# Shorter VectorE loop body, query factors turned in narrow transposes and moved as whole rows, and a new order of steps

## The chip, the cores and the metric

One core of one Trainium2 chip (trn2). The metric is device time in microseconds of one execution.

## The reference

x has 32 batches of 256 rows of 256 columns, the context 77 rows per batch. The first half is a cross attention of 8 heads of 128, without a softmax over keys: each head mixes a cosine similarity with a product of variance ratios, with weights that a small network takes from global means. The second half is a 16-head attention of head size 16 with a softmax, two normalisations and a gelu.

```python
dots = einsum('hqnd,hqmd->hqnm', f_q, f_k)
cosine_sim = dots / (qn[..., :, None] * kn[..., None, :])
q_ratio = 2.0 * minimum(q_var, 1.0) / (q_var + 1.0)
k_ratio = 2.0 * minimum(k_var, 1.0) / (k_var + 1.0)
var_component = einsum('hqn,hqm->hqnm', q_ratio, k_ratio)
mixed = cw * cosine_sim + vw * cosine_sim * decorr_scale + ww * var_component
out = einsum('hqnm,hqmd->hqnd', mixed, f_v)          # then @ w_out.T + b_out
x = x + tanh(g_xattn) * out
...
attn = softmax(scores)                                # 16 heads, over 256 rows
z = l2norm(l2norm(attn_out @ Wo) @ Wff)
x = x + tanh(g_ffn) * gelu(z)
```

## The kernel before, in words

A first phase (to about 235 us) prepares weights, context statistics and the mixing weights. The main phase (`main_phase`) works on 16 pairs of batches (512 rows each) in turns. Products of f32 values are made of three f16 matmuls (`products`, L861 to L863) on a high and a low half of each operand.

`ORDER` (L922) is a list of some 300 step names, written out by hand or by a program outside the kernel. Every engine walks through the same list and issues its own part of each step (`run`, with `a_part` and `b_part`). A turn has steps of three pairs: with `lead` 0 and 1 those of the first half and the projections, with `lead` 2 the softmax of the pair before. Turns 2 to 15 are one loop on the chip (`eng.Fori`, 14 turns, 13 branches back, line L1121); the turns at both ends are written out.

The steps that the text names:

- `q0`..`q7`: queries on TensorE; VectorE takes their statistics into `qst` (L1550, `bn_stats`).
- `qs1` (VectorE): moments of `qst` into `qft` (L871 to L882), variance ratios, times a weight, into `aux` (L1563). `qpow` (GpSimd, L1481): `rq`, inverse norms. `qs2` (VectorE, L1567): `rq` times a factor, into `aux`.
- `a0` (TensorE, L1286): one transpose of `aux`, 128x128. ScalarE copies 32 rows to `sqT` (L1394) and 32 to `wqT` (L1395), VectorE makes the low half of `wqT` (L1530).
- `aux` (SyncE, SP queue): stores `sqT` to DRAM as `sq_rows` (L1166), then loads `wqT` into one row group of `mT` in 8 small pieces (L1169).
- `sqe` (SP queue, L1178): 12 DMAs, each broadcasting a head's row of `sq_rows` over up to 77 partitions of `sqE`.
- `fk`, `G`, `V`: keys, keys times weights, values times weights; `.h` is the copy of the high half on ScalarE, `.l` the low half on VectorE.
- `d0`..`d5` (TensorE): dots. `d.o` (VectorE, L1580): `md` = dots times `sqE`. `m.h`, `m.l`: `mT`. `y0`, `y1`: the sum over keys; `y.o` adds x.
- `ln1`, `lpow`, `ln2` (`norm`, L1604), `zz`, `pq`, `pk`, `pv` (`v`, L1420): layer norm, transposes and projections of the second half. `ql`, `kl` are low halves on VectorE (L1537).
- `parts`, `back0`, `back1` (SP queue): q and k go to DRAM and come back stacked by heads as `qstack`, `kstack` (2 x 16 DMAs, L1205).
- `S` (TensorE, L1334), `M` (VectorE, L1624, row maxima `nm`), `X` (ScalarE, L1435, exponentials `prob` and their `sums`), 32 each a turn over three banks; `R` (VectorE: reciprocal `rs`, L1632, and `vsp`, L1638), `P` (TensorE, L1346), `E`, `L`, `O`, `F`: the rest of the attention. F4 (L1654) makes `zb`.

The results of all steps but S and P share three PSUM banks (`work`) in the turn of the list; a step waits until the bank's user three steps before has been drained (`wait_drained`, `wait_filled`).

Of the kernel before, what the change touches and what calls it, by code (L numbers as in the profile page):

```python
# [52 lines left out]
def build(nc, x, ctx_in, g_x, g_f, ln_g, ln_b, w_in, w_inT, w1T, b1, wln_g, wln_b, w2T, b2, w_outT, b_out,  # L53
# [812 lines left out]
def moments(nc, link, k0, st, ft, scale=1.0):  # L866
# [57 lines left out]
a0.h M5 S6 V2 X4 a0.l R0 aux M6 V1.h S7 P0 X5 V1.l M7 V2.h S8 X6 G3 M8 G4 V2.l X7 S9 V3 M9 G3.h ldx G4.h ldy G3.l X8
ldr R1 S10 V4 M10 V3.h G4.l X9 sqe V3.l S11 V5 V4.h M11 S12 X10 P1 V4.l M12 X11 S13 G5 M13 V5.h S14 G5.h fk0 V5.l E0
R2 X12 G5.l fk1 M14 X13 z fk0.h S15 P2 X14 M15 S16 S17 fk0.l d0 X15 M16 fk1.h M17 S18 X16 d1 fk1.l R3 X17 M18 S19 d2
L0 X18 M19 S20 P3 M20 X19 d0.o S21 S22 d1.o m0.h d3 M21 X20 m0.l d4 X21 R4 d2.o m1.h M22 S23 m2.h P4 E1 m1.l X22 m2.l
S24 d3.o d5 d4.o m3.h S25 zT0 M23 m4.h y0 m3.l zT0.h M24 X23 d5.o M25 m5.h X24 m4.l m5.l X25 S26 L1 S27 y1 M26 zT0.f
M27 X26 y0.o zT0.l X27 R5 R6 O0 y1.o ln1 S28 zT1 O0. S29 fk2 zT1.h P5 M28 lpow fk2.h zT1.f M29 P6 ln2 X28 S30 X29 S31
fk2.l zz0 M30 zz1 zz0.h zT1.l O1 zz1.h zz0.l X30 M31 q0 zz1.l X31 pk0 O1. R7 q0.o E2 P7 L2 pq0 E3 pk0.h L3 pk0.l pk1  # L930
pq0.h pq0.l pq1 pk1.h pk1.l O2 pq1.h pq1.l O3 O2. parts q1 O3. q2 F1 q1.o q3 q2.o back0 F2 q4 q5 q3.o F3 q4.o q6 q5.o
# [41 lines left out]
def main_phase(nc, ctx, w, x_rows, out_rows, rk_rows, kr_rows, sq_rows, fixed_rows, parts):  # L973
# [717 lines left out]
```

## Time and profile before

| | us |
|---|---|
| median of 3 runs | 1545.91 (1535.48 to 1546.38) |
| the profiled execution | 1539.16 |
| its span | 1537.4 |
| mean granted TensorE clock | 0.963 |
| busy: TensorE, VectorE, ScalarE, GpSimd | 1308.2, 1155.9, 1019.8, 199.5 |
| DMA | 125.05 MB in 182906 packets |

All times in rows are of the one profiled execution, from the start of its span. A row of the timeline gives the start, how long it took, the engine, line, operation and tile, and in brackets how long the engine was idle before it and what released it.

### The profile page before, as it was taken

The numbers are of one execution on the slowest core, as the hardware profiler recorded it, in microseconds if no ns is written. First come the engines' busy times: TensorE is split into PE (matmuls) and PEld (weight loads), VectorE is DVE, ScalarE is ACT, GpSimd is POOL, SyncE is SP. The second block draws the span as 40 slices with busy tenths as digits, with TensorE's granted clock in tenths as the row PEclk, the third lists the DMA queues.
The fourth block names the chain that finished last, engine by engine and source line by source line (L and its number), as shares of the span: only waits on it lengthen the run. The fifth ranks groups of instructions, "written<-read, shape, count | busy, mean of one in ns | idle before, by whom it ended". The sixth has DMA issues, their size and how long they took to land.

```text
span 1537.4 us, 35793 instructions
## 1 busy us (share of the span) xinstructions
PE 1308.2 (85%) x10706; PEld 868.5 (56%) x10706; DVE 1155.9 (75%) x3191; ACT 1019.8 (66%) x3381; POOL 199.5 (13%) x129
## 2 busy tenths in 40 slices
PE   5988756889898989898989898989898989898855
PEld 2655635465656565656565565656565656574622
DVE  5878465577877887878787787878787969696845
ACT  5564112276777777777777777768686868685767
POOL 2441031000101010101010101010101010101000
PEclk9999868999999999999999999999999999999978
DMA  8420002261616160716160807161616162626160
GB/s 255 139 91 17 3 10 63 53 107 40 134 38 134 33 138 28 138 33 137 34 131 13 148 24 144 28 138 34 126 46 115 56 111 61 111 61 111 49 110 15
DMA packets 182906, 125.05 MB, mean 81 GB/s; under 512 B 16430, under 2 KB 180431, under 8 KB 182800
## 3 DMA queue, kind: packets, MB, share of 16 engines
q1 hardware_dynamic: 182800, 124.00, 37.1%
q14 instruction: 84, 0.69, 0.2%
q8 instruction: 22, 0.36, 0.1%
HBM read 87.00 MB, written 25.77 MB: 73 GB/s over the span
## 4 chain that ended last, share of the span: by engine, by line
PE 32%; SPq 18%; DVE 12%; issue 12%; DMA 7%; ACT 3%; DVEq 0%; POOL 0%; POOLq 0%; ACTq 0%
PE work L861 9%; PE work L863 9%; PE work L862 9%; SPq L1178 7%; SPq L1169 5%; DMA sqE<-sq_rows 4%; SPq L1205 3%; DVE nm L1624 3%; PE attended L1346 2%; ACT prob L1435 2%; DMA qstack<-parts 2%; PE score L1334 2%; PE work L1241 1%; DVE l2s L1594 1%; DMA parts<-kl 1%
## 5 line engine op out<-in xcount | busy, mean ns | idle before, releaser
L1435 ACT ACTIVATE prob<-score,nm 128x256 f32<-128x256 f32 x1024 | 484.3, 514 | 30.9 <-DVE nm L1624 28.8
L1624 DVE TENSOR_REDUCE nm<-score 128x2 f32<-128x512 f32 x512 | 339.1, 682 | 36.8 <-PE score L1334 34.2
L1334 PE MATMUL score<-qstack,kstack 128*128 128x256 f16 x1024 | 193.8, 280 | 92.4 <-ACT prob L1435 45.9
L1435 ACT ACTIVATION_READ_ACCUMULATOR prob<-score,nm 128x1 f32 x1024 | 252.5, 247 | 0.0
L1334 PEld LDWEIGHTS score<-qstack,kstack 128*128 128x128 f16 x1024 | 80.0, 99 | 177.3 <-ACT prob L1435 111.1
L1550 DVE BATCH_NORM_STATS2 qst<-work 128x6 f32<-128x128 f32 x512 | 112.4, 284 | 68.7 <-PE work L863 68.7
L1346 PE MATMUL attended<-prob,vsp 128*32 128x256 f32 x2048 | 135.7, 388 | 1.4 <-DVE vsp L1638 1.4
L861 PE MATMUL work<-woutTh,fvph 128*128 128x256 f16 x384 | 105.8, 275 | 13.4 <-ACT v L1420 13.1
L1481 POOL TENSOR_TENSOR rq<-qft,mhalf 128x32 f32<-128x32 f32 x16 | 86.8, 5428 | 226.6 <-DVEq L1558 226.6
L861 PE MATMUL work<-xTh,Gh 128*128 128x256 f16 (+1 forms) x320 | 89.5, 280 | 28.3 <-DVE md L1580 28.3
L862 PE MATMUL work<-woutTl,fvph 128*128 128x256 f16 x384 | 105.5, 275 | 0.0
L863 PE MATMUL work<-woutTh,fvpl 128*128 128x256 f16 x384 | 105.5, 275 | 0.0
L1485 POOL TENSOR_TENSOR l2r<-l2v,mhalf 128x4 f32<-128x4 f32 x16 | 16.1, 1007 | 665.3 <-DVE l2v L1597 665.3
L861 PE MATMUL work<-wTh,xTh 128*128 128x512 f16 x256 | 98.1, 383 | 3.9 <-DVE xTl L1544 1.9
L862 PE MATMUL work<-wTl,xTh 128*128 128x512 f16 x256 | 98.0, 383 | 0.0
L863 PE MATMUL work<-wTh,xTl 128*128 128x512 f16 x256 | 98.0, 383 | 0.0
L1388 ACT ACTIVATE Vph<-work,rkc 128x256 f16<-128x256 f32 (+1 forms) x160 | 73.9, 525 | 30.5 <-PE work L863 30.5
L862 PE MATMUL work<-xTl,Gh 128*128 128x256 f16 (+1 forms) x320 | 89.4, 280 | 0.0
L863 PE MATMUL work<-xTh,Gl 128*128 128x256 f16 (+1 forms) x320 | 89.3, 279 | 0.0
L861 PE MATMUL work<-Vph,mTh 128*128 128x256 f16 (+1 forms) x320 | 87.3, 273 | 1.6 <-issue 0.2
L863 PE MATMUL work<-Vph,mTl 128*128 128x256 f16 (+1 forms) x320 | 87.1, 272 | 0.0
L862 PE MATMUL work<-Vpl,mTh 128*128 128x256 f16 (+1 forms) x320 | 87.0, 272 | 0.0
(327 smaller groups left out, 3288.9 us busy)
## 6 DMA issues: line engine op xcount, KB each, us to landing
kstack<-parts SPq DMA_DIRECT2D x256, 64.0 KB, 4.0
qstack<-parts SPq DMA_DIRECT2D x256, 64.0 KB, 4.2
sqE<-sq_rows SPq DMA_DIRECT2D x64, 154.0 KB
s_xin<-in_x SPq DMA_DIRECT2D x8, 1024.0 KB, 6.0
xin<-in_x SPq DMA_DIRECT2D x16, 512.0 KB, 3.4
x2S<-in_x SPq DMA_DIRECT2D x16, 512.0 KB, 4.7
x<-x2S SPq DMA_DIRECT2D x16, 512.0 KB, 4.1
out<-zb SPq DMA_DIRECT2D x16, 512.0 KB, 5.2
```

The costliest lines, as they stand in the source:

```text
L861: nc.tensor.matmul(out, a["h"][at], b["h"][bt], start=first, stop=False)
L862: nc.tensor.matmul(out, a["h"][at], b["l"][bt], start=False, stop=False)
L863: return nc.tensor.matmul(out, a["l"][at], b["h"][bt], start=False, stop=last)
L1169: sp.dma_start(mT[half][KR_ROW:KR_ROW + H, t // 2, HT - 1, t % 2 * P:(t % 2 + 1) * P], wqT[half][(PT + t) * H:(PT + t + 1) * H, :]).then_i ...
L1178: sp.dma_start(sqE[lo:hi, t, :].rearrange("p (t n) -> p t n", n=P), sq_rows[:, h, :].partition_broadcast(hi - lo)).then_inc(sq_in, 16)
L1334: last = nc.tensor.matmul(sc[n % SC][:, jj * NQ:(jj + 1) * NQ], kstack[:, e, j, b2 * NQ + k * P:b2 * NQ + (k + 1) * P], qstack[:, j, b2 * ...
L1346: last = nc.tensor.matmul(pvb[t][32 * j:32 * j + 32, 0:NQ], vsp[:, e, k, j, :], prob[:, n % PG, k, j, :], start=(e == 0 and k == 0), stop= ...
L1388: last = nc.scalar.activation(dst, src, ACT.Copy, scale=scale)
L1435: nc.scalar.activation(prob[:, g % PG, k, u % 4, :], sc[n % SC][:, jj * NQ:(jj + 1) * NQ], ACT.Exp, bias=nm[:, u:u + 1], accum_out=sums[:, ...
L1481: nc.gpsimd.tensor_tensor(rq[:], qft[:, 0, :, :], w["mhalf"][:].rearrange("p (t h) -> p t h", h=H), ALU.pow).then_inc(rq_ready, 1)
L1550: last = nc.vector.bn_stats(qst[:, t, 4 * half + h, :], bank(e)[:, h * DH:(h + 1) * DH])
L1624: nc.vector.tensor_reduce(nm[:, 2 * n:2 * n + 2], sc[n % SC][:, :].rearrange("p (u q) -> p u q", q=NQ), AX.X, ALU.max, negate=True).then_i ...
```

## The change

- Waits that VectorE's, GpSimd's and other engines' own order already covers are left out: of several names in `wait_drained` the last only, `sq_in` and `y_in` once a pair, `init` once. One copy in `moments` and its link go, and `rs` is written over `sums`. VectorE's loop body goes from 318 to 307 instructions, and the instructions written ahead of it become 6 fewer (counted in the two built programs).
- `aux` has two planes instead of four, and a plane is turned by 4 transposes of [128x8] into [8 x 512]: `a1` for the ratios (`wqT`), `a0` for the factors (`sqT`). `sqT` and `wqT` have 8 partitions of 512 values instead of 32 of 128.
- `sq_rows` is [8, 512]: a broadcast reads one piece of 2 KB for each partition instead of four of 512 bytes. The 8 small loads of `wqT` become 2, in a step `wq` of their own.
- A new `ORDER`, with 47 users of the three banks instead of 46.

```diff
-    sq_rows = nc.dram_tensor("sq_rows", (PT, H, P), F32, kind="Internal").ap()
+    sq_rows = nc.dram_tensor("sq_rows", (H, PR), F32, kind="Internal").ap()
...
-    link(k0 + 4, nc.vector.tensor_copy(ft[:, 5, :, :], ft[:, 1, :, :]))
...
-    aux, sqT, wqT = sb("aux", [P, 4, PT, H]), sb("sqT", [PT * H, P]), pair("wqT", [2 * PT * H, P])
+    aux, sqT, wqT = sb("aux", [P, 2, PT, H]), sb("sqT", [H, PR]), pair("wqT", [H, PR])
...
                     sp_wait_drained(a, "a0")
-                    sp_wait_filled(a - 1, "y0", "y1")
-                    sp.dma_start(sq_rows.rearrange("t h n -> (t h) n"), sqT[:]).then_inc(sq_stored, 16)
+                    sp_wait(sq_in, a * SQ_LOADS * 16)
+                    sp.dma_start(sq_rows, sqT[:]).then_inc(sq_stored, 16)
+                elif step == "wq":
+
+                    sp_wait_drained(a, "a1")
+                    sp_wait_filled(a - 1, "y1")
                     for half in "hl":
-                        for t in range(PT):
-                            sp.dma_start(mT[half][KR_ROW:KR_ROW + H, t // 2, HT - 1, t % 2 * P:(t % 2 + 1) * P],
-                                         wqT[half][(PT + t) * H:(PT + t + 1) * H, :]).then_inc(wq_in, 16)
+                        sp.dma_start(mT[half][KR_ROW:KR_ROW + H, :, HT - 1, :],
+                                     wqT[half][:].rearrange("h (b n) -> h b n", b=2)).then_inc(wq_in, 16)
...
-                            sp.dma_start(sqE[lo:hi, t, :].rearrange("p (t n) -> p t n", n=P),
-                                         sq_rows[:, h, :].partition_broadcast(hi - lo)).then_inc(sq_in, 16)
+                            sp.dma_start(sqE[lo:hi, t, :], sq_rows[h, :].partition_broadcast(hi - lo)).then_inc(sq_in, 16)
...
-                    pe.wait_ge(wqr_ready, a + 1)
-                    pe.wait_ge(sq_ready, a + 1)
-                    last = nc.tensor.transpose(bk[:, 0:P], aux[:].rearrange("p s t h -> p (s t h)"), ident[:])
+                    pe.wait_ge((sq_ready, wqr_ready)[c], a + 1)
+                    for t in range(PT):
+                        last = nc.tensor.transpose(bk[0:H, t * P:(t + 1) * P], aux[:, c, t, :], ident[:])
...
-                    wait_drained(dve, a, *(f"q{n}" for n in range(2 * PT)))
-
-                    wait_filled(dve, a - 1, "a0")
-                    dve.wait_ge(init, 5)
+                    wait_drained(dve, a, f"q{2 * PT - 1}")
+
+                    wait_filled(dve, a - 1, "a1")
...
-                    dve.wait_ge(sq_in, a * SQ_LOADS * 16 + SQ_LOADS * 16)
+                    if c == 0:
+                        dve.wait_ge(sq_in, a * SQ_LOADS * 16 + SQ_LOADS * 16)
```

The head of the list and its tail, before and after:

```diff
-rk qs1 V0 qpow S0 G0 V0.h M0 S1 S2 G0.h G1 M1 X0 V0.l X1 G0.l S3 G2 M2 G1.h S4 M3 V1 G2.h X2 G1.l G2.l X3 qs2 S5 M4 a0
+rk V0 qs1 G0 V0.h S0 qpow V1 G0.h M0 V0.l X0 G0.l S1 V1.h a1 M1 S2 S3 a1.h M2 G1 X1 V1.l G1.h M3 V2 ldr X2 a1.l S4
...
-q7 q6.o pv0 q7.o F4 pv1 pv0.v res pv1.v out back1
+q4 q3.o q5 q4.o q6 q5.o F4 q7 q6.o res pv1 back1 q7.o pv1.v out
```

On the SP queue, at the start of the loop body (behind the loads of `back1` of the turn before), the store of `sqT` and what stands between it and the broadcast. Before:

```order
L1166 DMA sq_rows<-sqT 32x128
L1169 DMA mTh<-wqTh 8x128 x4
L1169 DMA mTl<-wqTl 8x128 x4
L1156 ISA
L1156 DMA xin<-in_x 128x4x256
L1139 REGISTER_ALU
L1161 ISA
L1161 DMA x2S<-in_x 128x4x256
L1184 ISA
L1184 DMA Vph<-kr_rows 8x2x256
L1184 ISA
L1184 DMA Vpl<-kr_rows 8x2x256
```

After:

```order
L1185 ISA
L1185 DMA Vph<-kr_rows 8x2x256
L1185 ISA
L1185 DMA Vpl<-kr_rows 8x2x256
L1138 ISA x2
L1165 DMA sq_rows<-sqT 8x512
L1138 REGISTER_ALU
L1138 ISA
L1180 DMA sqE<-sq_rows 77x512
```

The loads of x and of `wqT` now stand behind the 12 broadcasts, the `kr_rows` loads ahead of the store.

On VectorE, the end of what stands ahead of the first `md` of a turn (ISA and REGISTER_ALU set registers for waits). Before:

```order
L1621 TENSOR_TENSOR oTl<-attended,oTh 128x256
L1623 REGISTER_ALU
L1624 TENSOR_REDUCE nm<-score 128x2
L1623 REGISTER_ALU
L1624 TENSOR_REDUCE nm<-score 128x2
L1049 REGISTER_ALU
L1574 ISA
L1579 ISA
L1580 TENSOR_TENSOR md<-work,sqE 128x512
```

After:

```order
L1641 TENSOR_TENSOR vsp<-v,sums 128x8x16
L1626 REGISTER_ALU
L1627 TENSOR_REDUCE nm<-score 128x2
L1048 ISA
L1576 ISA
L1581 ISA
L1582 TENSOR_TENSOR md<-work,sqE 128x512
```

In the whole turn 21 row maxima (`nm`) stand ahead of the first `md` before, 15 after.

On ScalarE, the end of the exponentials (`prob`) of a turn. Before:

```order
L1435 ACTIVATE prob,sums<-score,nm 128x256 x2
L1452 ACTIVATE junk,nrm<-work 128x256 x2
L1454 ACTIVATE zb<-work 128x256
L1049 REGISTER_ALU
L1441 ACTIVATE oTh<-attended 128x256
L1438 REGISTER_ALU
L1441 ACTIVATE oTh<-attended 128x256
L1049 REGISTER_ALU
L1405 REGISTER_ALU
L1407 ACTIVATE kh<-work 128x512
```

After:

```order
L1437 ACTIVATE prob,sums<-score,nm 128x256 x2
L1407 REGISTER_ALU
L1409 ACTIVATE kh<-work 128x512
L1048 REGISTER_ALU
L1409 ACTIVATE kh<-work 128x512
L1048 REGISTER_ALU
L1443 ACTIVATE oTh<-attended 128x256
```

The group of O1 (`junk`, `zb`) went ahead of the last exponentials, and both `kh` stand right behind them, since TensorE computes pk0, pk1 and pq0 ahead of P7.

## Rows read from the trace of the kernel before

**Rows 1.** Table by stretches: 13 turns of the loop, then one turn's two parts.
```profile
384.40:1402.70 1018.30, 922.11 (x8023) 614.58 (x8021) 814.12 (x2186) 752.23 (x2561) 108.39 (x65) 0.99 0.40 84
...
core 0: us, PE busy (x) PEld busy (x) DVE busy (x) ACT busy (x) POOL busy (x), PEclk, DMA share, GB/s
1020.90:1071.60 50.70, 46.22 (x461) 33.74 (x462) 46.40 (x106) 44.85 (x166) 4.50 (x2) 1.00 0.34 63
1071.60:1099.20 27.60, 24.39 (x157) 13.24 (x155) 16.23 (x63) 13.05 (x33) 3.86 (x4) 1.00 0.49 121
```
**Rows 2.** Waits, of the turn 1013.4 to 1091.6; the last row of the whole span.
```profile
PE score L1334 <- ACT prob L1435: 2.9, 4, 1.8
PE work L861 <- DVE md L1580: 1.5, 1, 1.5
PE work L861 <- ACT v L1420: 0.9, 1, 0.9
PE work L1241 <- DVE norm L1604: 0.5, 1, 0.5
...
DVE qft L871 <- issue: 50.4, 13, 4.2
```
**Rows 3.** Timeline of the hand-over between two turns.
```profile
1045.52 1.07 PE L1346 MATMUL attended<-prob,vsp 128*32 128x256 f32 x16
...
1071.04 0.47 ACT L1435 ACTIVATE prob<-score,nm 128x256 f32<-128x256 f32 x1
1071.95 0.29 DVE L1638 TENSOR_TENSOR vsp<-v,rs 128x128 f32<-128x128 f32 x1
1074.20 0.59 ACT L1407 ACTIVATE kh<-work 128x512 f16<-128x512 f32 x1
1078.51 0.69 DVE L1537 SCALAR_TENSOR_TENSOR ql<-work,qh 128x512 f16<-128x512 f32 x1 [0.60 <-ACT qh L1407]
1096.95 0.39 PE L1334 MATMUL score<-qstack,kstack 128*128 128x256 f16 x2 [2.14 <-DMA qstack<-parts]
1099.17 0.47 ACT L1435 ACTIVATE prob<-score,nm 128x256 f32<-128x256 f32 x1 [0.62 <-DVE nm L1624]
```
**Rows 4.** The chain to `md`: tile, DMA, queue and timeline, 1020 to 1050.
```profile
L1394 ACT ACTIVATE sqT<-work x1: 267/267/267, 1025.6 to 1025.6; 32x128 f32<-32x128 f32 x1
DMA to landing us min/median/max: 3.9/3.9/3.9
...
DMA packets 3097, 1.75 MB, mean 146 GB/s; under 512 B 137, under 2 KB 3097, under 8 KB 3097
q1 hardware_dynamic: 3097, 1.75, 52.6%
...
1035.98 7.74 SPq L1178 DMA_DIRECT2D sqE<-sq_rows  x12
1043.38 4.73 DMA sqE<-sq_rows
1048.23 1.29 DVE L1580 TENSOR_TENSOR md<-work,sqE 128x512 f32<-128x512 f32 x2 [1.62 <-DMA sqE<-sq_rows]
```
**Rows 5.** Timeline of VectorE behind the branch.
```profile
1017.28 0.21 DVE L871 TENSOR_TENSOR qft<-qst 128x32 f32<-128x32 f32 x1 [3.92 <-issue]
1019.99 0.19 DVE L1563 TENSOR_TENSOR aux<-qft,wwv 128x32 f32<-128x32 f32 x1
```
**Rows 6.** Timeline of ScalarE behind the same branch.
```profile
1014.53 1.28 ACT L1388 ACT_TABLE_LOAD   x1
```
**Rows 7.** Timeline of VectorE where the loop is left.
```profile
1404.46 0.21 DVE L871 TENSOR_TENSOR qft<-qst 128x32 f32<-128x32 f32 x1
```
**Rows 8.** DMA queues: packets, MB, share; the span, the turn, 1089.2 to 1089.7.
```profile
q14 instruction: 84, 0.69, 0.2%
...
q14 instruction: 5, 0.04, 0.3%
...
q14 instruction: 1, 0.01, 14.3%
```
**Rows 9.** The chain of waits in the hand-over, two of its steps.
```profile
1079.36 0.22 PE work L862
...
1089.07 0.22 PE work L862
```

More of the change, by code:

```diff
@@ L913 @@
 SC_CREDIT = SCORES
-A_STEPS, B_STEPS = 12, GROUPS + 5
+A_STEPS, B_STEPS = 11, GROUPS + 5
 ORDER = """
-rk qs1 V0 qpow S0 G0 V0.h M0 S1 S2 G0.h G1 M1 X0 V0.l X1 G0.l S3 G2 M2 G1.h S4 M3 V1 G2.h X2 G1.l G2.l X3 qs2 S5 M4 a0
[L924 to L931, printed above, removed]
-q7 q6.o pv0 q7.o F4 pv1 pv0.v res pv1.v out back1
+rk V0 qs1 G0 V0.h S0 qpow V1 G0.h M0 V0.l X0 G0.l S1 V1.h a1 M1 S2 S3 a1.h M2 G1 X1 V1.l G1.h M3 V2 ldr X2 a1.l S4
+V2.h qs2 S5 G1.l X3 a0 V2.l G2 M4 G3 a0.v M5 G2.h S6 aux X4 V3 R0 M6 G3.h G2.l X5 S7 P0 M7 V3.h G3.l G4 X6 sqe V3.l S8
+G5 G4.h M8 S9 X7 V4 G4.l M9 X8 R1 S10 X9 S11 M10 P1 G5.h X10 G5.l S12 V5 M11 ldy V4.h M12 S13 wq d0 X11 V4.l ldx V5.h
+M13 S14 X12 d1 V5.l R2 X13 M14 S15 P2 d0.o X14 M15 S16 m0.h d1.o fk0 M16 m0.l S17 fk0.h d2 E0 fk0.l d3 X15 M17 m1.h
+d2.o S18 X16 d4 m1.l M18 X17 R3 S19 d5 m2.h M19 X18 S20 m2.l P3 d3.o X19 d4.o fk1 m3.h M20 m3.l X20 S21 S22 z y0 m4.h
+fk1.h d5.o L0 m5.h M21 E1 R4 X21 M22 zT0 S23 m4.l X22 P4 fk1.l zT0.h m5.l S24 y0.o S25 y1 zT0.f M23 L1 X23 M24 M25 X24
+R5 X25 zT0.l zT1 y1.o O0 zT1.h ln1 S26 O0. S27 P5 zT1.f M26 lpow O1 M27 X26 ln2 X27 S28 S29 M28 O1. zz0 zz1 zT1.l
+zz0.h S30 R6 fk2 zz1.h zz0.l X28 P6 zz1.l fk2.h M29 S31 pk0 M30 X29 M31 X30 fk2.l pk1 X31 pq0 pk0.h R7 pk1.h pk0.l P7
+E2 pq0.h pk1.l L2 pq1 pq0.l E3 L3 O2 pq1.h pq1.l O3 O2. parts q0 O3. q1 F1 q0.o pv0 q1.o back0 F2 q2 pv0.v q3 q2.o F3
+q4 q3.o q5 q4.o q6 q5.o F4 q7 q6.o res pv1 back1 q7.o pv1.v out
 """.split()
@@ L1186, in a_part @@
                 elif step == "parts":
-                    sp_wait_drained(a, "pq0", "pq1", "pk0", "pk1")
+                    sp_wait_drained(a, "pq1", "pk1")
                     for landed in stack_in:
@@ L1469, in _ @@
             nc.gpsimd.memset(kstack[:], 0.0).then_inc(init, 1)
-            nc.gpsimd.memset(aux[:], 0.0).then_inc(init, 1)
             def a_part(e, a):
@@ L1525, in a_part @@
                     drain(last, e)
-                elif e == "a0" and part == "l":
+                elif e == "a1" and part == "l":
                     done = HALVES[lead(e)]
                     dve.wait_ge(hi_ready[lead(e)], a * len(done) + done.index(e) + 1)
-                    rows = slice(PT * H, 2 * PT * H)
-                    drain(nc.vector.scalar_tensor_tensor(wqT["l"][rows, :], bank(e)[rows, 0:P], MS, wqT["h"][rows, :],
+                    drain(nc.vector.scalar_tensor_tensor(wqT["l"][:], bank(e)[0:H, :], MS, wqT["h"][:],
                                                          ALU.mult, ALU.subtract), e)
@@ L1628, in b_part @@
                     units = slice(8 * n, 8 * n + 8)
-                    if n == 0:
+                    if n == 0 and isinstance(b, int) and b == 0:
                         dve.wait_ge(init, 3)
                     dve.wait_ge(exp_done, b * 2 * SCORES + 8 * n + 8 + EXP_CREDIT)
-                    link(n + 1, nc.vector.reciprocal(rs[:, units], sums[:, units]))
+                    link(n + 1, nc.vector.reciprocal(sums[:, units], sums[:, units]))
                     if n == 0:
-                        wait_drained(dve, b, "pv0", "pv1")
+                        wait_drained(dve, b, "pv1")
                     dve.wait_ge(pv_done, b * GROUPS + n - 1 + PV_CREDIT)
```

65 lines of the change are left out of this document (34 added, 31 removed).

## The prediction

> **What bounds the kernel now.** The page's shares (TensorE 85% busy, VectorE 75%, ScalarE 66%) are averages over unlike stages, so the table by stretches comes first [rows 1]. The 13 turns between the first and the last branch of the main loop take 1018.3 us, 78.3 us a turn; divided by 13, TensorE is busy 70.9 us of it, VectorE 62.6, ScalarE 57.9. TensorE's clock is granted at 0.99 of full speed, 2.4 GHz, there. No engine is full, yet the turn splits into two unlike parts: from the first to the last exponential of a turn (50.7 us) ScalarE works 44.85 us and TensorE 46.2; from the last exponential to the first of the next turn (27.6 us) ScalarE works 13. The turn is thus a loop of two stretches: a dense one, in which TensorE and ScalarE are both nearly full, and a hand-over.
>
> The table of waits of one turn [rows 2] names what opens the gaps on TensorE: 2.9 us for exponentials, 1.5 for `md`, 0.9 for ScalarE's `v`, 0.5 for `norm`, and in the timeline 2.1 for the stacked queries (qstack) [rows 3]. VectorE waits 1.6 us for `sqE` [rows 4] and, in the timeline, 3.9 us for nothing ("issue") from 1013.37 on, before it begins the statistics `qft` at 1017.28 [rows 5]. That is the loop's branch. ScalarE takes the same branch without a gap: its table load, the first work of a new turn, has no idle time before it [rows 6]. When VectorE leaves the loop instead of branching back, the same `qft` begins with no idle time either [rows 7]. So the 3.9 us belong to the taken branch on VectorE alone; 13 of them sum to 50.4 us [rows 2].
>
> **Does the shorter program remove that stall?** In a turn 5 instruction packets arrive, of about 8.2 KB (0.69 MB in 84) [rows 8]. A narrow window places one just before VectorE's branch at 1089.2 to 1089.7 [rows 8]. Counted along VectorE's instructions in the trace, it lies at the 314th of the 318 of the loop, and another at the 186th, 128 apart. My reading: the body just reaches into a fourth block of 128 instructions, whose entry pushes the first block out. The new body has 307 instructions, and 6 went ahead of it, so the boundary should fall at the 320th, behind the end. All 5 packets a turn would go: the 84 should fall to about 20.
>
> The Trainium skill (Runtime: NRT & Kernel Launch, section on instruction fetch) has a store of 512 instructions, refilled in blocks of 256, and a branch out of the two-block window fetches. The trace agrees with the kind of stall but not with the block, since its packets are 8.2 KB. By blocks of 256, 307 instructions could still straddle three, and nothing would change; that is the first rival, whose time is worked out there from rows.
>
> **The edits and their price, for one turn.**
> (1) Stall and copy. `qft` to `aux` took 2.9 us [rows 5]; one copy of about 0.2 goes. All of it then runs while TensorE computes V0 and G0. Now the first exponential stands 2.25 us behind the first score (1096.95 to 1099.17), because the row maximum waits behind `qft` [rows 3, 5]; score 0.4, maximum 0.68 and hops give 1.35. Gain 0.9 us. The rest of the stall was covered: the first score waits for qstack until 1096.95 anyway, which is why 3.9 us removed are not 3.9 us gained.
> (2) Tail order. From the end of the last exponential (1071.51) to the end of `ql` (1079.20) it is 7.7 us, as TensorE then still has P7, three projections and their evacuations before it [rows 3]. In the new order pk0, pk1 and pq0 run before P7, and ScalarE's copies follow the exponentials at once. What is left behind the last exponential: `vsp` ready after 0.7, P7 1.0, pq1 (6 matmuls of 0.216; 45 such stand between the two rows of the chain [rows 9]) 1.3, copy 0.6, residual 0.7, hops 0.2 [rows 3]: 4.5 us. Gain 3.2. From `ql` to the first score 17.75 us pass [rows 3]: 4 stores, their landing, 16 loads at 0.45, the last landing. Nothing in it changes. From the end of pq1 TensorE has O2, O3, q0 to q7 (60 matmuls at 0.216), pv0, pv1 and V0 (39 of half the columns, 0.108) and G0 (0.6) to do, 17.8 us; `ql` ends 1.4 us behind pq1, so qstack comes at 19.2 and TensorE waits 1.4 us, where it waited 2.1 and 0.9 for `v` [rows 2, 3].
> (3) Added in the dense stretch: one square-and-copy group (O1) moves into it, 1.2 us of ScalarE (two squares, two reads, a copy, each 0.2 to 0.4); the two copies of 0.27 us on 32x128 become two of [8x512], not seen before, bounded by 0.27 and by the 0.6 of a 128x512 copy [rows 3, 4]; I take 0.6, as free length is what it has in common: +0.6. Together +1.8. Four narrow transposes instead of one, twice, cost TensorE some 0.3 to 0.9 us; it has that much idle behind the exponentials at this place.
> (4) The chain to `md`. Now: store of sqT, eight small loads, two of x, two of kr, then 12 issues for `sqE` from 1035.98, last landing 1048.11, `md` 1048.23, 34.9 us behind the end of `zb` [rows 4]. New, from the end of pv1 on TensorE: the SP queue is through its 16 loads, `out` and two kr loads at about 12; sqT is copied at about 11.8, behind four pairs of exponentials and six evacuations; its store lands 3.9 later [rows 4], at 16. Then 12 `sqE` issues. They took 12.1 us to the last landing, in packets of 512 B; new rows are 2 KB. From below: no issue held up (half of the 7.74 us of now, 4) and the last landing of 4.7 as now, 8.7 [rows 4]. From above: no gain, 12.1; that no packet of 2 KB was seen leaves this end open, and rival B takes it up. I take 10, nearer to above since the bytes are the same. So `sqE` stands at 26, between 25 and 28.5. But the order asks for it sooner: 15 maxima come before the first `md`, not 21, and I put that at 25 (first score 3.6, first exponential 1.35 later, 14 pairs at the 0.95 that two steps of `prob` take, 6.7 of evacuations). The wait is 1 to 1.5, where it was 1.6 to 2.0 [rows 4]: gain 0.5. The eight small loads and the x loads leave this chain; that pays for the earlier place.
> The Trainium skill (DMA: Bandwidth & Descriptors, section on why a DMA increments by 16) says that a DMA runs on the largest number up to 16 that divides its outer dimension. With 77, 51, 76 rows the load is uneven, and by that rule one DMA engine moves 84 of the rows. The trace shows only the average: 3097 packets and 52.6% of 16 engines over 12 us, 0.033 us each [rows 4]. By the rule 84 rows of four such packets take 11 us, between my value and the upper end; what a packet of 2 KB takes, no run here shows yet.
> (5) Waits dropped on other engines, `rs` written over `sums`, one memset less: nothing; they are waits already met, hidden under busy engines. If one was not redundant in time, another wait of the same chain stands in its place.
> (6) `norm` to zz0: 5.0 us of TensorE work cover it where 5.5 did, so its gap of 0.5 [rows 2] grows to 1.0: loss 0.3 (half falls into ScalarE's work).
>
> (7) The wait of 0.9 for `v` at V0 goes with the 47th bank user; it lies beside the wait for qstack: 0 by itself. But ScalarE has 5.85 us idle in the dense stretch [rows 1], 2 of them at `md`; banks that come free earlier and a first exponential that no longer lags can return between 0 and 2 of the rest, and I count 0.5.
>
> Sum for a turn: -0.9 - 3.2 + 1.8 - 0.5 + 0.3 - 0.5 = -3.0. The profiled execution took 1539.16 us with a span of 1537.4; 14 turns give 42, the turns at the edges another 2: 1495. The runs shown (1535 to 1546, median 1545.9) lie 4 to 7 us around and above that execution, so a median of 1497 is my figure. One per cent, 15 us, is about what a measurement here can tell from no change.
>
> **Rivals.**
> A. The stall stays, because a boundary still falls inside the new body. `qft` then ends 6.6 us behind pv1 and not 2.8, the first maximum 2.5 us late: -3.0 + 2.5 = -0.5 a turn, 1532. For it: the positions are inferred. Against: 13 instructions of room. Chance 0.09. The block rule quoted above leads here.
> B. Slower: the chain to `md`. If the broadcast of 2 KB rows out of one DRAM row took longer than the 12.1 us of now, every us beyond 10 is a us of turn, since VectorE stands at `md` with the maxima behind it and ScalarE starves. The gain of 3.0 is eaten at 13 us, slower by 1% at 14.1; at 16 it costs +3.0, 1581. For it: `md` is asked for six maxima earlier, and the store leaves from 8 partitions, not 32. Against: same bytes, a fourth of the packets. 0.05.
> C. Order gives back: `sqE` at 28.5 (+3 of wait), or the last exponentials, now after pk0 and pk1, hold P7: -0.5 to -1.3 a turn, about 1524. 0.16.
> D. More: ScalarE's other idle time in the dense stretch shrinks by its full 2 instead of 0.5, and half of the cost in (3) is covered as well: -5, 1467. 0.16.
> My forecast, -2 to -4 a turn (1482 to 1510): 0.54.
>
> Range: 1466 to 1532, from D to A. Faster by over 1% (below 1523): forecast, D and half of C, 0.78; within 1%, A and the other half of C: 0.17; slower, B: 0.05.
>
> **What would show it.** VectorE idle "issue" before `qft` gone; instruction packets near 20, none in a turn; the first exponential 1.4 us behind the first score; `ql` 4.5 us behind the last exponential; `sqE` landed about 10 us behind its first issue, `md` waiting about 1 us. Turns of 75.3 us. I am wrong if `qft` still waits, if `md` waits over 3 us, or if the dense stretch grows by more than 2 us.

## The result and the profile after

The changed kernel takes 1453.36 us (median of 4 runs, 1447.33 to 1455.04), the kernel before 1541.24 us beside it (4 runs, 1535.48 to 1546.38): ratio 0.9424, 95% interval 0.9372 to 0.9475. The forecast was 1497 us in a range of 1466 to 1532: the sign was right, the size was not, and the time lies below the range. The profiled execution took 1452.54 us, with a span of 1450.8.

The page of the changed kernel, busy times and DMA queues:

```profile
PE 1305.6 (90%) x10818; PEld 878.3 (61%) x10818; DVE 1138.5 (78%) x3171; ACT 1023.9 (71%) x3381; POOL 199.1 (14%) x128
...
q1 hardware_dynamic: 151392, 124.00, 30.8%
q8 instruction: 22, 0.36, 0.1%
q14 instruction: 19, 0.16, 0.0%
```

TensorE and ScalarE do the same work as before; what went is idle time. Queue q14 has 19 packets where it had 84 [rows 8].

The table by stretches: the 13 turns of the loop, then the dense stretch and the hand-over of one turn (us, busy time of each engine, granted clock, DMA share, GB/s):

```profile
375.06:1324.69 949.63, 917.20 (x8114) 622.78 (x8113) 806.37 (x2172) 756.16 (x2561) 108.41 (x65) 1.00 0.34 90
963.66:1013.80 50.14, 47.80 (x481) 35.36 (x479) 46.20 (x106) 46.38 (x171) 4.39 (x2) 1.00 0.27 71
1013.80:1036.30 22.50, 22.50 (x148) 12.62 (x146) 15.82 (x62) 11.77 (x28) 3.92 (x4) 1.00 0.44 134
```

Against [rows 1]: a turn takes 949.63 / 13 = 73.05 us instead of 78.33. In the hand-over TensorE is now busy all of 22.50 us, where it had 3.2 us of gaps in 27.60. In the dense stretch ScalarE is busy 1.5 us longer than before (46.38 against 44.85) in a stretch that is 0.6 shorter: its idle time fell from 5.85 to 3.76 us. This turn is a good one: over the 13 turns ScalarE's busy time there rose from 44.8 to 46.4 us and its idle time fell from 5.9 to 4.1.

Waits of one turn (959.5 to 1032.2), then of the whole span the wait of `md`:

```profile
PE work L861 <- DVE Vpl L1525: 0.8, 1, 0.8
PE score L1335 <- ACT prob L1437: 0.6, 2, 0.5
PE work L1242 <- DVE norm L1607: 0.5, 1, 0.5
PE work L861 <- DVE md L1582: 0.4, 1, 0.4
```

```profile
DVE md L1582 <- DMA sqE<-sq_rows: 16.7, 13, 2.4
```

Against [rows 2]: 2.9 for exponentials became 0.6, 1.5 for `md` 0.4, and the waits for `v` and `qstack` are gone. A wait of 0.8 for `Vpl`, the low half of V on VectorE, is new. `norm` did not grow to the 1.0 that step 6 of the prediction feared. The row `qft <- issue` has gone from the waits.

The timeline of VectorE at the branch, and of the hand-over:

```profile
958.35 1.68 DVE L1550 BATCH_NORM_STATS2 qst<-work 128x6 f32<-128x128 f32 x8
960.15 0.21 DVE L871 TENSOR_TENSOR qft<-qst 128x32 f32<-128x32 f32 x1
...
1013.28 0.49 ACT L1437 ACTIVATE prob<-score,nm 128x256 f32<-128x256 f32 x1
1013.73 1.11 ACT L1409 ACTIVATE kh<-work 128x512 f16<-128x512 f32 x2
1014.83 1.07 PE L1347 MATMUL attended<-prob,vsp 128*32 128x256 f32 x16
1017.97 0.69 DVE L1537 SCALAR_TENSOR_TENSOR ql<-work,qh 128x512 f16<-128x512 f32 x1 [1.00 <-ACT qh L1409]
```

`qft` follows `qst` at once, where it stood 3.92 us idle [rows 5]. `kh` follows the last exponential at once, and `ql` ends 4.9 us behind it, not 7.7 [rows 3].

These steps, as means over the 13 turns (from the starts and lengths of the instructions named, in the timeline of each turn), beside the forecast by the prediction's own terms:

| us | before | forecast | after |
|---|---|---|---|
| end of last exponential to end of `ql` | 7.70 | 4.5 | 4.89 |
| end of `ql` to first score | 17.64 | 17.75 | 16.43 |
| first score to first exponential | 2.33 | 1.35 | 1.23 |
| first to last exponential | 50.66 | 51.8 | 50.51 |
| turn | 78.33 | 75.3 | 73.05 |

The first and third line came nearly as forecast. The second and fourth hold the missing 2.3 us a turn. The rest of the miss lies outside the 13 turns: of the 86.6 us that the two profiled executions differ by, 13 turns hold 68.7, one more turn of the loop 5.3, and the edges 12.7, where the prediction had 2.

### The profile page after: what moved, and what is told of

Its sections match the earlier page's. It is cut to its first block, busy times and chain, and to the rows that moved or that the text cites. A ratio compares the mean times of both kernels' runs of the same rounds, so it can differ in the third digit from the quotient of the medians.

```text
span 1450.8 us, 35577 instructions
## 1 busy us (share of the span) xinstructions
PE 1305.6 (90%) x10818; PEld 878.3 (61%) x10818; DVE 1138.5 (78%) x3171; ACT 1023.9 (71%) x3381; POOL 199.1 (14%) x128
## 4 chain that ended last, share of the span: by engine, by line
PE 38%; DVE 18%; issue 14%; ACT 6%; DMA 5%; SPq 3%; DVEq 1%; POOL 1%; ACTq 0%; POOLq 0%
PE work L861 10%; PE work L863 10%; PE work L862 10%; DVE nm L1627 5%; DMA sqE<-sq_rows 4%; PE attended L1347 4%; ACT prob L1437 3%; DVE mTl L1537 3%; PE score L1335 2%; SPq L1180 2%; DVE md L1582 2%; PE work L1242 1%; DVE l2s L1597 1%; DVE norm L1607 1%; DVE norm L1518 1%
## 5 line engine op out<-in xcount | busy, mean ns | idle before, releaser
L1437 ACT ACTIVATE prob<-score,nm 128x256 f32<-128x256 f32 x1024 | 473.2, 480 | 44.6 <-DVE nm L1627 40.4
L1437 ACT ACTIVATION_READ_ACCUMULATOR prob<-score,nm 128x1 f32 x1024 | 216.7, 212 | 0.0
L1335 PE MATMUL score<-qstack,kstack 128*128 128x256 f16 x1024 | 186.0, 277 | 28.4 <-ACT prob L1437 19.2
L1347 PE MATMUL attended<-prob,vsp 128*32 128x256 f32 x2048 | 139.4, 390 | 4.0 <-DVE vsp L1641 3.2
L1335 PEld LDWEIGHTS score<-qstack,kstack 128*128 128x128 f16 x1024 | 86.6, 98 | 87.7 <-ACT prob L1437 55.5
L861 PE MATMUL work<-woutTh,fvph 128*128 128x256 f16 x384 | 105.0, 273 | 13.7 <-DVE Vpl L1525 12.7
L1422 ACT ACTIVATE v<-work 128x512 f32<-128x512 f32 x32 | 19.1, 597 | 130.4 <-PE work L863 130.4
L1347 PEld LDWEIGHTS attended<-prob,vsp 128*32 128x32 f32 x2048 | 53.9, 110 | 56.9 <-DVE vsp L1641 17.4
## 6 DMA issues: line engine op xcount, KB each, us to landing
s_xin<-in_x SPq DMA_DIRECT2D x8, 1024.0 KB, 6.0
```

The costliest lines, as they stand in the source:

```text
L861: nc.tensor.matmul(out, a["h"][at], b["h"][bt], start=first, stop=False)
L1335: last = nc.tensor.matmul(sc[n % SC][:, jj * NQ:(jj + 1) * NQ], kstack[:, e, j, b2 * NQ + k * P:b2 * NQ + (k + 1) * P], qstack[:, j, b2 * ...
L1347: last = nc.tensor.matmul(pvb[t][32 * j:32 * j + 32, 0:NQ], vsp[:, e, k, j, :], prob[:, n % PG, k, j, :], start=(e == 0 and k == 0), stop= ...
L1437: nc.scalar.activation(prob[:, g % PG, k, u % 4, :], sc[n % SC][:, jj * NQ:(jj + 1) * NQ], ACT.Exp, bias=nm[:, u:u + 1], accum_out=sums[:, ...
```

## Experiments

Medians of the kernel before beside these runs were 1538.9 to 1540.9 us; ratios are to it, with their 95% intervals.

### The stall of VectorE: where the code lies, or how long it is

**Only the waits of VectorE's program left out** (order, layout and the rest as before; body of 311 instructions).

```diff
-                    dve.wait_ge(sq_in, a * SQ_LOADS * 16 + SQ_LOADS * 16)
+                    if c == 0:
+                        dve.wait_ge(sq_in, a * SQ_LOADS * 16 + SQ_LOADS * 16)
```

and the same for `q0` to `q7`, `y_in` and `init`. Expected:

> The kernel before, with only the waits left out of VectorE's program that its own order covers (loop body 311 instructions instead of 318, 2 fewer ahead of it); order, layout of aux and all else as before. Theory of the prediction (step 1 less its copy): the 3.9 us of issue idle before qft go, 84 instruction packets fall to about 20, and of the 3.9 us about 0.9 a turn come back as time, since the first score waits for qstack anyway: 13 us less, ratio about 0.99. Rival: the stall holds the whole hand-over (VectorE late at qft, at the maxima and at the banks behind them), 2.5 to 3.9 us a turn: 35 to 50 us less, ratio 0.977 to 0.967.

Measured: 1523.01 us, ratio 0.9898 (0.9866 to 0.9929); q14 19 packets, no issue idle before `qft`. It gains 16 us, 1.2 a turn: the prediction's 0.9 was near, the rival's 2.5 to 3.9 was not. Of the 1.2, 0.8 lie between the first score and the first exponential, where the prediction had them, and 0.6 ahead of the first score (17.05 us behind `ql` instead of 17.64); the dense stretch takes 0.2 back.

**60 instructions ahead of the loop of the kernel before, the loop itself untouched.**

```diff
+            for _ in range(120):
+                dve.wait_ge(init, 1)
             run(dve, a_part, b_part)
```

(Two such waits share one instruction; the built program has 60 more.)

> The kernel before with nothing changed inside the loop: 60 instructions that only wait for something long done are put ahead of VectorE's loop. Theory of the block: the stall hangs on where the 318 instructions lie against boundaries 128 apart; 60 more ahead move the boundaries from the 58th, 186th and 314th to the 126th and 254th, the body no longer reaches a fourth block: issue idle before qft gone, instruction packets about 20, time as in e1_prune within 5 us. Rival of the length: a body of 318 is too long wherever it lies: 3.9 us of idle before qft and 84 packets stay, time as before, up to 4 us more for the 60 instructions.

Measured: 1520.98 us, ratio 0.9899 (0.9864 to 0.9935), the same gain as with the shorter body. Of its page:

```profile
q14 instruction: 20, 0.16, 0.0%
```

With 318 instructions in the body and 60 more ahead, the stall is gone. It hangs on where the body lies, not on how long it is.

**16 and 8 instructions ahead of the loop of the changed kernel**, by the same edit with 32 and with 16 waits:

> The changed kernel with nothing changed inside the loop: 16 instructions that only wait for something long done go ahead of VectorE's loop. Theory of the block: 64 + 16 + 307 = 387 instructions pass the boundary at 384, the stall comes back: idle of 3 to 4 us before qft in each turn, 4 to 5 instruction packets a turn (about 84 in all), and the time grows by what a stall costs in the new order, 2.5 us a turn as the prediction priced it (35 us, ratio to the changed kernel 1.024). Rival of the length: 307 fits wherever it lies: no stall, at most 1 us more.

> As the run with 16 ahead, but 8 instructions: 64 + 8 + 307 = 379, under the boundary at 384. Theory of the block: no stall, about 20 packets, the time of the changed kernel within 2 us. Rival (any added instruction, or another place in the store, disturbs it): an idle before qft and tens of us more here too.

Measured with 16: 1480.76 us, ratio 0.9644 (0.9599 to 0.9689). With 8: 1447.32 us, ratio 0.9408 (0.9379 to 0.9437), no more than the changed kernel's time. The queue on the page and the group of `qft`, with 16 ahead:

```profile
q14 instruction: 84, 0.69, 0.2%
```

```profile
L871 DVE TENSOR_TENSOR qft<-qst 128x32 f32<-128x32 f32 x16 | 3.5, 217 | 31.8 <-PE work L863 23.2 <-issue 8.4
```

and the same group in the changed kernel:

```profile
L871 DVE TENSOR_TENSOR qft<-qst 128x32 f32<-128x32 f32 x16 | 3.5, 218 | 1.8
```

All 84 packets are back with 16, none with 8 (19). So a boundary lies where it was counted. The prediction put it at the 320th instruction, which is 384 behind a boundary that lies 64 instructions ahead of the body: 64 + 16 + 307 passes 384, 64 + 8 + 307 does not. The row with 31.8 us also shows how a releaser is misread: it names TensorE for 23.2 of them, though the same edit with 8 instructions ahead leaves next to no idle there; TensorE's last release only fell into the time in which VectorE stood. The stall costs more in the new order, (1480.76 - 1453.36) / 14 = 2.0 us a turn, because nothing covers it any more: the first score no longer waits for qstack, and the first exponential stands 3.43 us behind it instead of 1.23.

### Order, and the pieces of sq_rows

**The tail of the order turned back** (pk0, pk1 and pq0 behind the last exponentials and P7):

```diff
-P6 zz1.l fk2.h M29 S31 pk0 M30 X29 M31 X30 fk2.l pk1 X31 pq0 pk0.h R7 pk1.h pk0.l P7 E2 pq0.h pk1.l L2 pq1 pq0.l E3 L3 O2
+P6 zz1.l fk2.h M29 S31 M30 X29 M31 X30 fk2.l X31 pk0 R7 E2 P7 L2 pq0 E3 pk0.h L3 pk0.l pk1 pq0.h pq0.l pq1 pk1.h pk1.l O2
```

> The changed kernel with one edit in its order: pk0, pk1 and pq0 go back behind the last exponentials and P7, as before. Prediction's step 2: the end of the last exponential to the end of ql grows from 4.9 to about 7.7, all of it on the path: 2.8 us a turn, 39 us more in all. Rival: qstack no longer ends the hand-over in the changed kernel, it lands about 1.5 us before TensorE asks for it; then 2.8 later costs 1.3 a turn, 18 us, and the first score waits for qstack again.

Measured: 1492.53 us, ratio 0.9697 (0.9662 to 0.9732); 39 us more than the changed kernel. `ql` ends 7.83 us behind the last exponential, and from there the first score comes 16.42 behind as before the edit. That is what step 2 of the prediction says of the tail, nearly to the number. The rival falls: 16.4 us is TensorE's own work between pq1 and the first score (17.8 less the 1.4 by which `ql` follows pq1, as the prediction counted), and it all starts later when pq1 does.

**sq_rows in pieces of 512 bytes**:

```diff
-    sq_rows = nc.dram_tensor("sq_rows", (H, PR), F32, kind="Internal").ap()
+    sq_rows = nc.dram_tensor("sq_rows", (PT, H, P), F32, kind="Internal").ap()
...
-                            sp.dma_start(sqE[lo:hi, t, :], sq_rows[h, :].partition_broadcast(hi - lo)).then_inc(sq_in, 16)
+                            sp.dma_start(sqE[lo:hi, t, :].rearrange("p (t n) -> p t n", n=P),
+                                         sq_rows[:, h, :].partition_broadcast(hi - lo)).then_inc(sq_in, 16)
```

> The changed kernel with sq_rows in pieces of 512 bytes, as before, under the same store and the same 12 broadcasts at the same place. Prediction's term: first issue to last landing about 11 us with 2 KB rows, 12.1 with 512 bytes: md waits 1 us longer, 1 us a turn, 14 us more in all. Rival 1 (the packets count, not the bytes: issues of 0.64 instead of 0.35 us and four times the packets): 3 us a turn or more, over 40 us. Rival 2: nothing, within 3 us, as the bytes are the same and the wait at md is hidden.

Measured: 1469.6 us, ratio 0.9555 (0.9525 to 0.9585), 16 us more, 1.2 a turn. The wait of `md`, to set beside 16.7:

```profile
DVE md L1583 <- DMA sqE<-sq_rows: 34.2, 14, 3.9
```

From the first issue to `md` it is 12.6 us with 512 bytes and 11.3 with 2 KB (means of 13 turns): the term that the prediction put at 10 and expected to be 12.1 with 512 bytes.

**Everything but the order** (the order of before, with a0 split into a1 and a0, and `wq` behind `aux`):

```diff
-rk qs1 V0 qpow S0 ... X3 qs2 S5 M4 a0 a0.h M5 S6 ... a0.l R0 aux M6
+rk qs1 V0 qpow S0 ... X3 qs2 S5 M4 a1 a0 a1.h a0.v M5 S6 ... a1.l R0 aux wq M6
```

> The changed kernel (shorter VectorE program, aux in two planes, narrow transposes, 2 KB rows) with the order of before: only a0 becomes a1 and a0 side by side, and the step wq stands right behind aux. The prediction's steps: stall and copy -1.2 a turn by the run e1_prune, sqE earlier by 1 to 2 us where md waits 1.6 to 2.0 (-1.5), two longer copies +0.6: about -2.1 a turn, 1510 us, and the order gives the rest, 3 to 4 us a turn. Rival of the layout: it gives more than half of the 5.3, below 1495 us. The 16 loads of qstack and kstack landed 4.1 us (median) behind their issue before and 2.9 in the changed kernel, for no reason seen so far: if the layout (tiles at other addresses) does it, the median is 2.9 here; if the order does it, 4 to 5.

Measured: 1498.74 us, ratio 0.9734 (0.9697 to 0.9771), 24 us less than with the shorter program alone, and between the expected 1510 and the rival's 1495. No step of the prediction holds such a gain for the layout. The group of the stack loads gave the hint, here before, then this run:

```profile
DMA to landing us min/median/max: 2.7/4.2/6.9
```

```profile
DMA to landing us min/median/max: 2.2/3.0/3.9
```

### The addresses of the stacks

The 16 loads of a half stack write rows of 512 bytes into qstack and kstack. In the kernel before these tiles begin at 173696 and 181888 bytes of a partition, 128 past a multiple of 256; in the changed kernel, since `aux`, `sqT` and `wqT` have other sizes, at 176384 and 184576, which are multiples of 256. DMA queues during the loads of the first half, 1085.5 to 1094.0 before and 1024.0 to 1031.2 after:

```profile
q1 hardware_dynamic: 2137, 0.97, 73.8%
```

```profile
q1 hardware_dynamic: 2120, 0.97, 46.9%
```

The same 0.97 MB in the same number of packets: 8.5 us x 16 engines x 0.738 / 2137 = 0.047 us a packet before, 7.2 x 16 x 0.469 / 2120 = 0.025 after.

**Tiles moved, in the kernel before and in the changed one.** Four runs, of which nothing but addresses changes:

```diff
+    sb("shift", [P, 544])                       # 2176 bytes, ahead of x2S
+    sb("shift", [P, 32])                        # or 128 bytes, ahead of qstack
+    sb("shift", [P, 512])                       # or 2048 bytes, ahead of qstack
```

and in the changed kernel `rq` (128 bytes) moved from ahead of x2S to behind kstack.

> The kernel before with an unused tile of 2176 bytes a partition ahead of x2S, so that x2S, qh to kl, v, qstack, kstack, prob and what follows lie 2176 bytes higher; nothing else. If the addresses are what made the last 8 loads of a stack slow (packets of 512 bytes took 60 to 90 ns there, 27 in the changed kernel) and the exponentials slower (514 against 480 ns), this changes the landing median of 4.1 us or the mean of prob. If the order or what runs beside does it: landing, prob and time as before within noise.

> The kernel before with 128 unused bytes a partition right ahead of qstack: qstack and kstack start at a multiple of 256 bytes (173824, 182016) instead of 128 past one, and x2, prob and what follows move by 128 too; qh to kl stay where they were. Theory of alignment to 256 bytes: it is enough; the packets of 512 bytes of the last 8 loads fall from 60 to 90 ns to about 27, landing median 2.8 to 2.9 us, ql to the first score 15.5 instead of 17.6, time -15 to -20 us as with the 2176 bytes. Rival (a large shift does it, or the source tiles qh to kl do): packets, landing and time as before.

> The kernel before with 2048 unused bytes ahead of qstack: qstack and kstack move far but stay 128 past a multiple of 256. Theory of alignment: nothing changes, packets of 60 to 90 ns, landing median 4.1 or more, time as before within 5 us. Rival (the place in memory, whatever its alignment): packets of 27 ns and 15 to 20 us less.

> The changed kernel with rq (128 bytes) moved behind kstack: x2S, qh to kl, v, qstack and kstack start 128 bytes lower, so 128 past a multiple of 256 as in the kernel before; nothing else changes. Theory: the slow packets return, qstack lands some 17.1 to 17.7 us behind ql instead of before 16.4, the first score waits for it, and of the 1.4 us a turn that the prediction had there 0.7 to 1.4 come back: 11 to 22 us more, about 1465 to 1475 us. Rival: the new order hides it, within 5 us of the changed kernel.

| kernel | stacks past a multiple of 256 | us | ratio to before |
|---|---|---|---|
| before, 2176 bytes ahead of x2S | 0 | 1519.74 | 0.988 (0.985 to 0.9909) |
| before, 128 bytes ahead of qstack | 0 | 1525.52 | 0.9929 (0.9893 to 0.9965) |
| before, 2048 bytes ahead of qstack | 128 | 1539.05 | 0.9998 (0.998 to 1.0017) |
| changed, rq behind kstack | 128 | 1500.74 | 0.9765 (0.9736 to 0.9794) |

Landing of the stack loads, first 128 bytes, then 2048 bytes:

```profile
DMA to landing us min/median/max: 2.2/2.8/3.8
```

```profile
DMA to landing us min/median/max: 2.6/4.2/6.1
```

A shift of 128 bytes does it, one of 2048 does not: of these places it is the ones at a multiple of 256 bytes that are fast. Whether the tiles qh to kl, moved too by the 2176 bytes, add to it stays open; the two intervals overlap.

The last run is the telling one: the whole change with unaligned stacks takes 1500.74 us, 47 more than the changed kernel. The forecast was 1497, but 1465 to 1475 was expected of this run, so the size of the loss was a surprise. Its loss does not lie at the first score (16.68 us behind `ql` instead of 16.43), where the prediction had looked. First the DMA queues during the loads of the second half (990 to 996: share of the engines in 40 slices, then the queue), then the timeline of the SP queue behind them and of `md`:

```profile
DMA  9999999999999999999999999999999999999999
...
q1 hardware_dynamic: 1583, 0.72, 127.1%
```

```profile
997.24 0.28 SPq L1165 DMA_DIRECT2D sq_rows<-sqT  x1
1001.56 4.31 SPq L1180 DMA_DIRECT2D sqE<-sq_rows  x12
...
1012.97 0.69 DVE L1582 TENSOR_TENSOR md<-work,sqE 128x512 f32<-128x512 f32 x1 [3.68 <-DMA sqE<-sq_rows]
```

The same chain in the changed kernel:

```profile
970.07 0.28 SPq L1165 DMA_DIRECT2D sq_rows<-sqT  x1
971.75 4.23 SPq L1180 DMA_DIRECT2D sqE<-sq_rows  x12
...
982.83 0.69 DVE L1582 TENSOR_TENSOR md<-work,sqE 128x512 f32<-128x512 f32 x1 [0.72 <-DMA sqE<-sq_rows]
```

All DMA engines are full (packets overlap in the record, hence 127%) with the slow loads of the second half. The store of sqT is queued behind them and lands 4.3 us later (997.24 to 1001.56) instead of 1.7, `sqE` starts later by as much, and `md` waits 56.4 us in the span instead of 16.7:

```profile
DVE md L1582 <- DMA sqE<-sq_rows: 56.4, 14, 5.2
```

Over the 13 turns `md` comes 3.2 us later behind the first store of q and k, and a turn takes 3.4 us more (76.42).

**The order of before with unaligned stacks**, to see whether the two gains add:

```diff
-    rq = sb("rq", [P, PT, H])
...
+    rq = sb("rq", [P, PT, H])
     x2 = sb("x2", [P, PT, DIM])
```

> All edits but the order, with rq moved behind kstack so that the stacks keep their place 128 past a multiple of 256: stall, copy, aux layout and 2 KB rows without order and without alignment. If alignment is what e5_old_order gained beyond the stall (1499 against 1523): the time is 1515 to 1522 us here, and the order alone, at equal alignment, is worth 15 to 21 us (to 1501) instead of 47. Rival: alignment pays only in the new order, and this stays near 1500.

Measured: 1529.2 us, ratio 0.9931 (0.991 to 0.9952). With the three others:

| us | stacks 128 past | stacks aligned |
|---|---|---|
| order of before | 1529.2 | 1498.7 |
| new order | 1500.7 | 1453.4 |

The two do not add: alignment gives 30 us in the old order and 47 in the new one, the order 28 or 45. The layout by itself, unaligned and in the old order, gains nothing over the shorter program alone (1529.2 against 1523.0, with intervals that just overlap): the wait at `md` falls from 25.9 to 3.4 us in the span, but the dense stretch grows from 50.87 to 52.48 us a turn. Half of that is work: ScalarE is busy 45.5 us there instead of 44.7, as the two longer copies of step 3 would have it (`sqT` takes 0.57 us instead of 0.27). Beside it stands a wait that is new. In both runs that have all edits but the order, TensorE stands once a turn for 3.1 us at a V step of the dense stretch, some 8 us behind the first exponential:

```profile
PE work L861 <- DVE Vpl L1525: 50.9, 18, 3.1
```

With the shorter program alone this wait is 3.8 us in the span, in the changed kernel 12.7. The old order has the two transpose steps side by side, and so one more user of the three banks, without room made for it; that this is why TensorE waits is argued, not tested. If so, part of the 28 us of the order is room that it makes for the layout. The rival (alignment pays only in the new order) falls; the expected 1515 to 1522 was too low as well.

**Reciprocals over sums in the kernel before**, for the exponentials, which take 480 ns instead of 514 in the changed kernel:

```diff
-                    link(n + 1, nc.vector.reciprocal(rs[:, units], sums[:, units]))
+                    link(n + 1, nc.vector.reciprocal(sums[:, units], sums[:, units]))
```

> The kernel before with the reciprocals written over sums instead of into rs; nothing else. The exponentials took 514 ns and the reading of their sum 247 in the kernel before, 490 and 223 with all edits but the order, 480 and 212 in the changed kernel, and moving tiles did not change them. If rs matters (ScalarE adds into sums while VectorE reads it): below 500 and 235 here, and up to 1 us a turn less. Otherwise 512 to 516 and 245 to 248 and the time of before; the cause is then another edit and stays open.

Measured: 1537.61 us, ratio 0.9985 (0.9964 to 1.0006), exponentials 514 ns. It is not this, nor the alignment (514 with 128 bytes ahead), nor the 512-byte pieces (478). The cause stays open.

**A version that beats both.** In the changed kernel `sqE`, `md` and x2S still begin 64, 64 and 32 bytes past a multiple of 256. Small tiles given out in another order align them at no cost in space:

```diff
+    rk_all, l2m, st4 = sb("rk_all", [P, HT, NB]), sb("l2m", [P, PT, 2]), sb("st4", [P, PT, 2])
     sqE, md = sb("sqE", [P, HT, PR]), sb("md", [P, 2, PR])
...
+    l2s, l2t = sb("l2s", [P, PT, 6]), sb("l2t", [P, PT, 2])
+    l2v, l2r = sb("l2v", [P, PT]), sb("l2r", [P, PT])
+    x2S = sb("x2S", [P, PT, DIM])
```

> The changed kernel with tiles given in another order so that sqE, md and x2S too start at a multiple of 256 bytes (before this at 64, 64 and 32 past one); qstack and kstack stay where they are. If alignment matters for each DMA that writes there: 2 KB packets of sqE fall from 105 to 120 ns, md waits 0.5 to 1 us a turn less than its 1.2, the time falls by 5 to 14 us. Rival: only short packets, or loads that stand close together, suffer: packets and time as in the changed kernel within 3 us.

Measured: 1440.13 us, ratio 0.937 (0.9345 to 0.9396), 13 us less than the changed kernel, with a turn of 72.42 us.

```profile
DVE md L1583 <- DMA sqE<-sq_rows: 8.2, 10, 2.8
```

The time and the wait (0.6 us a turn less) are as expected, the packets only in part. While `sqE` alone is on the queues its packets of 2 KB take 106 ns with either address. Where the load of x2S runs beside it, packets of 1 KB fall from 68 to 61 ns and those of 2 KB from 119 to 110 (packets that overlap one of the other size, means of 13 turns), and `md` comes 0.5 us earlier behind the first issue. Three tiles moved at once; which of them pays, no run parts.

## Why the prediction was wrong in size

**Step 1, stall and copy (-0.9 a turn).** Right in kind and nearly in size: 16 us alone, 1.2 a turn. The limit of three blocks of 128, inferred from two packets, held in six placements: counted from the boundary ahead of it, the body ends at 388 and 387 in the two kernels that stall (before, and changed with 16 ahead), and at 379, 320, 371 and 379 in the four that do not. The Trainium skill (Runtime: NRT & Kernel Launch, section on instruction fetch) has blocks of 256 in a store of 512. The placements alone do not rule these out: if the body of before began not 70 but 198 behind a boundary, it would end at 516 there, at 515 with 16 ahead, and at 507 or less in the others. What the trace does not fit is the block. Every packet has 8192 bytes; in the loop they come one at a time, the 186th and the 314th instruction of the body get one each, and 5 come in a turn, an odd number. The block of 128 is shown by that, the limit of three such blocks is argued. The lag of the first exponential in the turn read was 2.22 us and not the 2.25 of the sum, which changes nothing. That the stall would be worth 2.0 in the new order was priced at 2.5 in rival A, nearly right too.

**Step 2, tail of the order (-3.2).** Right: -2.81, and 39 us back when it is undone. But the sentence behind it failed: "From `ql` to the first score 17.75 us pass ... Nothing in it changes", and so "TensorE waits 1.4 us". It is 16.43 us, and TensorE does not wait. Its own work was counted rightly (17.8, less the 1.4 by which `ql` follows pq1) and now sets the time. What was wrong is the arrival of `qstack`, taken from the trace of before as if it were fixed. There the first score, which waited for it, stood 17.64 us behind `ql`; it stands 17.05 behind with VectorE's shorter program alone and 16.54 with all edits but the order and the alignment. Alignment brings it to 14.59 in the old order. In the new one it is worth only 0.25 at this place (16.68 in the run with rq behind kstack), for there TensorE's own work covers the rest.

**Step 3 and 7, the dense stretch (+1.8 and -0.5).** ScalarE is busy 1.6 us more there, near the 1.8 forecast. The two copies measured 0.57 us each instead of 0.27, as the prediction took them; the exponentials, which nobody counted on, gave 0.6 back. What failed is step 7: "banks that come free earlier ... can return between 0 and 2 of the rest, and I count 0.5". Over the 13 turns ScalarE's idle time in the stretch fell by 1.8 us, of which `md` had 0.5, so the rest returned 1.3. That is the first half of rival D, which the prediction held at 0.16. It hangs on the alignment: with unaligned stacks the idle time is 7.2 us instead of 4.1, and the stretch grows by 3 us (53.61).

**Step 4, the chain to `md` (-0.5).** The 10 us from the first `sqE` issue to its landing measured about 11, as near as the two rows could give. The failing term stands ahead of it: "its store lands 3.9 later". From the store to the first `sqE` issue, which waits for it, 1.8 us pass in the changed kernel and 4.5 with unaligned stacks. That `md` waits 1.2 us a turn in the changed kernel, as forecast (1 to 1.5), is luck: 2.1 too much for the store and 1.3 too little for `sqE` partly cancel. With unaligned stacks it waits 3.9. That is the first mechanism of rival C ("+3 of wait"), which came true in the run with rq behind kstack, though not its time.

**Steps 5 and 6.** Nothing and at most 0.3: as forecast, `norm` even stayed at 0.5.

**The edges (-2).** Wrong by 11 us. The first branch comes at 375.06 instead of 384.39, 9.3 us sooner, of which one turn of the loop is 5.3; from the last branch to the end it is 126.1 us instead of 134.7, 8.6 less. The prediction gave the turns written out there 2 us without working them out. Which of their waits fell, no run here was made to show.

So the forecast of 1497 meets the 1500.74 of the change without its alignment, but not by right terms throughout: there a turn takes 76.4 us, 1.1 more than forecast, and the edges give 10 us more. What the forecast lacked first of all stands in no line of the diff as such: new sizes of small tiles move all tiles behind them. It is worth 47 us in the new order, and it made the store of `sqT` and the loads around it faster than any row of before could show. The prediction listed "two planes instead of four" and never asked for the addresses.

## What to carry to other kernels

Where an edit changes the size of a tile, write down the start addresses of all tiles that DMAs write in short rows, before and after, and try them at multiples of 256 bytes: here that was worth 13 to 47 us and cost nothing but the order of declarations, or 128 bytes. A landing time taken from a trace is good for the addresses, and for the queue around it, of that trace only. A stall of an engine at a loop's branch is tested with a few idle instructions ahead of the loop, without touching it.

## What the runs showed of the hardware that was not expected

- DMA writes of 512-byte rows into SBUF, 128 bytes past a multiple of 256: packets of 60 to 100 ns instead of 27, but not from the first. In the first 4 us of the loads of a first half they take 27 to 31 ns at either address, and the slow ones come behind these (means over 13 turns of the kernel before: 27, 27, 27, 31, 63, 91, 80 ns from us to us). The Trainium skill (DMA: Bandwidth & Descriptors, section on how a descriptor splits into AXI transactions) says that a transaction has at most 256 bytes and must start at a multiple of 256, so that a descriptor which starts elsewhere begins at the multiple below; it says so of reads, and here it is the rows written that lie off. The alignment that counts agrees with the trace. By that rule, as an estimate, 512 bytes at 128 past take three transactions where two stood, half more; the trace shows 1.9 times over the whole series and over 3 times in its slow part, and what makes that part slow no run here shows.
- VectorE's instructions come in blocks of 128 (8.2 KB a packet, 128 instructions apart). The bodies that lay within three of them fetched nothing in the loop (19 or 20 packets in the span); those that reached 3 or 4 instructions into a fourth fetched 5 packets in every turn (84) and stood 2 to 4 us at the branch. ScalarE, with a body of 225 instructions (297 records a turn, of which 72 read sums), never did; where it lies was not varied.
- The 2 KB packets of `sqE` take 109 ns (106 while they are alone), those of 512 bytes 30, so that four take 120: by the byte they are almost even. The 12 issues take 4.0 us instead of 7.5, yet from the first issue to `md` only 1.3 us are gained. Whether these come from the issues or from the tenth that the transfer is shorter, no run parts.
